# Two steps moved ahead of a wait in TensorE's order of an attention LSTM's turn

## The reference

```python
def attend(h):
    q = h @ Wq.T
    scores = jnp.einsum('bc,bsc->bs', q, context)
    alpha = jax.nn.softmax(scores, axis=-1)
    ctx = jnp.einsum('bs,bsc->bc', alpha, context)
    return jnp.tanh(jnp.concatenate([ctx, h], axis=-1) @ Wout.T + b_out)

def step(carry, x_t):
    h, c, attn = carry
    inp = jnp.concatenate([x_t, attn], axis=-1)
    gates = inp @ W_ih.T + b_ih + h @ W_hh.T + b_hh
    i, f, g, o = jnp.split(gates, 4, axis=-1)
    c = jax.nn.sigmoid(f) * c + jax.nn.sigmoid(i) * jnp.tanh(g)
    h = jax.nn.sigmoid(o) * jnp.tanh(c)
    out = attn_out = attend(h)
    return ((h, c, attn_out), out)
```

## Time and profile before

| | |
|---|---|
| median of 3 runs | 6059.23 us (6057.89 to 6060.78) |
| the profiled execution's own time | 6056.11 us |
| its span | 6054.3 us |
| PE busy | 5506.3 us, 91% of the span |
| PEld busy | 3879.1 us, 64% |
| DVE busy | 3606.7 us, 60% |
| ACT busy | 2103.8 us, 35% |
| POOL busy | 317.7 us, 5% |

### The profile page before, as it was taken

One profiled execution on the slowest core, in us unless ns is written; L12 is line 12 of the kernel. 1 busy time (PEld: TensorE's weight loads), 2 busy tenths in 40 slices (PEclk: granted clock), 3 DMA queues, 4 the chain that ended last, 5 costly groups with the idle time before them and its releaser, 6 DMA issues. The chain is left out here.

```text
span 6054.3 us, 385300 instructions
## 1 busy us (share of the span) xinstructions
PE 5506.3 (91%) x171736; PEld 3879.1 (64%) x171736; DVE 3606.7 (60%) x16290; ACT 2103.8 (35%) x8003; POOL 317.7 (5%) x779
## 2 busy tenths in 40 slices
PE   6899999999999999999999999999888879887989
PEld 2577777777777777777777777777644444444433
DVE  4355555555555555555555555555487898888831
ACT  3144444444444444444444444444222122223221
POOL 0000000000000000000000000000011111111000
PEclk8999999999999999999999999999899899899989
DMA  1100000000000000000000000000211101011111
GB/s 69 57 2 2 2 2 2 2 2 2 2 2 2 2 2 2 2 2 2 2 2 2 2 2 2 2 2 17 81 58 40 40 28 47 31 45 33 47 38 54
DMA packets 45135, 111.64 MB, mean 18 GB/s; under 512 B 8160, under 2 KB 10208, under 8 KB 44528
## 3 DMA queue, kind: packets, MB, share of 16 engines
q1 hardware_dynamic: 43600, 109.39, 5.6%
q10 hardware_dynamic: 1440, 1.06, 0.1%
HBM read 99.90 MB, written 10.52 MB: 18 GB/s over the span
## 5 line engine op out<-in xcount | busy, mean ns | idle before, releaser
L711 PE MATMUL lstm_part_ps<-lstm_keys,lstm_hid 128*4 128x128 f32 x32768 | 1024.1, 273 | 205.5 <-DVE lstm_hid L880 205.5
L727 PE MATMUL lstm_ctx_ps<-lstm_values,lstm_alpha 128*4 128x128 f32 (+1 forms) x49152 | 1051.4, 237 | 0.2 <-issue 0.2
L711 PEld LDWEIGHTS lstm_part_ps<-lstm_keys,lstm_hid 128*4 128x4 f32 x32768 | 771.3, 86 | 427.2 <-DVE lstm_hid L880 413.6
L727 PEld LDWEIGHTS lstm_ctx_ps<-lstm_values,lstm_alpha 128*4 128x4 f32 x49152 | 904.8, 86 | 90.7 <-issue 0.4
L909 DVE TENSOR_REDUCE lstm_neg_max<-lstm_part_ps 128x1 f32<-128x128 f32 x1024 | 299.1, 292 | 678.8 <-PE lstm_part_ps L711 678.8
L842 ACT ACTIVATE lstm_expo<-lstm_part_ps,lstm_neg_max 128x128 f32<-128x128 f32 x1024 | 376.4, 368 | 862.2 <-DVE lstm_neg_max L909 862.2
L670 PE MATMUL lstm_half_ps<-lstm_w_hid,lstm_hid 128*13 128x96 f32 x16384 | 596.0, 246 | 0.0
L862 DVE STREAM_TRANSPOSE lstm_gates<-lstm_half_ps 128x96 f32<-128x96 f32 x1026 | 290.1, 283 | 396.1 <-PE lstm_half_ps L670 372.0
L670 PE MATMUL lstm_half_ps<-lstm_w_attn,lstm_attn 128*13 128x96 f32 x16448 | 526.0, 248 | 0.0
L670 PEld LDWEIGHTS lstm_half_ps<-lstm_w_attn,lstm_attn 128*13 128x13 f32 x16448 | 300.5, 93 | 154.6 <-ACT lstm_attn L855 106.7
L1944 ACT ACTIVATE mix_gated<-mix_gate_ps 115x512 f32<-115x512 f32 (+2 forms) x200 | 112.6, 563 | 820.0 <-PE mix_gate_ps L1674 819.9
(11 more groups left out here) (336 smaller groups left out, 8593.0 us busy)
## 6 DMA issues: line engine op xcount, KB each, us to landing
mix_ring<-in_sm_chunks SPq DMA_DIRECT2D x120, 358.0 KB, 2.9
mix_ring<-in_mix_chunks SPq DMA_DIRECT2D x80, 384.0 KB, 3.0
lstm_xg<-xg_rows SPq DMA_DIRECT2D x514, 16.0 KB
xg_rows<-lstm_xg_tile SPq DMA_DIRECT2D x16, 512.0 KB, 2.6
ctxT<-in_ctxT SPq DMA_DIRECT2D x1, 2048.0 KB, 14.6
out_xT<-xT SPq DMA_DIRECT2D x4, 512.0 KB, 3.8
xT<-in_xT SPq DMA_DIRECT2D x1, 1536.0 KB, 9.8
lstm_w_x<-in_lstm_w_x SPq DMA_DIRECT2D x1, 1024.0 KB, 10.8
```

Of the source, the lines that this page charges most:

```text
L711: mm = pe.matmul(part_rows(score_ps[part], b), hid[:, k, lo:lo + SPACE], keys[:, k, b * SRC + c * P:b * SRC + (c + 1) * P], start=(n == 0 ...
L727: mm = pe.matmul(part_rows(ctx_ps[n], b), alpha[:, b, c, SPACE - 1 - c:2 * SPACE - 1 - c], values[:, b * SC + c, ctx_cols[n]], start=(c == ...
```

## The change

In `gates`, `half_attn(0, 1)` moves from behind `half_attn(1, 0)` to behind `half_attn(0, 0)`, and so ahead of the wait for `attn_ready[1]`. In the loop's body, `hidden_part()` moves from behind `turn(0)` to ahead of the wait for `exp_ready`. The instructions and their number stay the same, on all engines.

```diff
@@ -750,9 +750,9 @@
                     o_gate_x_hid(u)
                     pe.wait_ge(attn_ready[0], t + 1)
                     half_attn(0, 0)
+                    half_attn(0, 1)
                     pe.wait_ge(attn_ready[1], t + 1)
                     half_attn(1, 0).then_inc(half_ready[0], 1)
-                    half_attn(0, 1)
                     half_attn(1, 1).then_inc(half_ready[1], 1)
                     o_gate_attn()
 
@@ -783,9 +783,9 @@
                             scores(c, 0)
                         scores(2, 1)
                         scores(3, 1).then_inc(scores_ready, 1)
+                        hidden_part()
                         pe.wait_ge(exp_ready, 2 * t + 1)
                         turn(0)
-                        hidden_part()
                         half_hid(0, 0)
                         pe.wait_ge(alpha_ready, 2 * t + 1)
                         for n in range(PIECES):
```

## The result

The changed kernel takes 6080.13 us (median of 7 runs, 6078.34 to 6084.19) against 6059.23 us (7 runs, 6057.89 to 6060.78): ratio 1.0033, 95% interval 1.0024 to 1.0043. It is slower, by 20.9 us, or 0.041 us in each of the 512 turns. That lies in the range given (6040 to 6088), but not in its likeliest case, no change (6048 to 6071). The rival that said slower named the place rightly: a filler (a step put into an idle gap) makes the instruction behind it late.

The account below looks back on a forecast made before the run. The LSTM-with-attention loop, 512 turns of 7.73 us, was taken as the bound, followed along one turn's chain. Terms of 0 and +2.6 us added to the 6059.2 median gave 6061.8 us; 8-in-10 range 6040 to 6088.

Parts of the forecast that it names:

- no change: Whole kernel: the two moves cancel out within what a measurement can tell, 6048 to 6071 us; chance 0.60.
- The rival that said slower: At `turn(0)` and `half_attn(1, 0)`: filler outlasts its cover, from 0.024 us a turn; 6090 at 0.03 each; chance 0.23.
- Edit 1, 0 a turn: In `gates`, `half_attn(0, 1)` moved ahead of the wait for `attn_ready[1]`: second half and output gate earlier, nothing gained, 0 us.
- The rival that L867 had been held by the second transpose: VectorE's L867 waits for the second L862, not L831; part of the faster rival, 6028 to 6044 us, chance 0.15.
- The idle time only moves: TensorE's idle time goes from ahead of `turn(0)` to behind it, some 0.2 us a turn ahead of L727.
- The sign that I had set for being wrong on edit 2: Distance from the accumulator read's end to L886, 0.37 us before, changing by more than 0.02.
- No slack behind `turn(0)`: `turn(0)` releases copy L886, so any lateness delays the context, `turn(1)` and the rest of the turn equally.
- Edit 2, +0.005 a turn: `hidden_part()` moved ahead of the exponentials' wait: just fills the gap, `turn(0)` ends 0.005 us later, 2.6 us in all.
- The bound of +0.03: Upper bound per turn for moving `hidden_part()`, in us, from the last strip ending at 2005.37.
- saved start from rest: At `turn(0)`: 0.25 us from start to end, against 0.23 for `turn(1)` out of a busy array; refund offsets lateness.
- The start in the array's flow: Earlier matmuls delay the next by just what the array still has to do; `select(1)` starts at 2008.37, load at 2008.34.
- The strict order: `hidden_part`'s passes start one behind the other, `turn(0)` 0.395 us late, +202 us, 6261; chance 0.02.

Follow-up runs that it names:

- d_both_first: Kernel before, with `hidden_part()` and `half_hid(0, 0)` both moved ahead of the wait for the exponentials: 6145.63 us against 6057.37.
- b_hidden_only: Kernel before, with only `hidden_part()` moved ahead of the wait for the exponentials: 6076.69 us against 6057.37.
- c_halfhid_first: Kernel before, with `half_hid(0, 0)` instead of `hidden_part()` moved ahead of the wait for the exponentials: 6058.76 us against 6057.37.
- m_halfhid_narrow: Kernel before, with `half_hid(0, 0)` and the narrow pieces of `hidden_part` ahead of the exponentials' wait, wide ones behind `turn(0)`: 6146.32 us against 6060.69.
- l_halfhid_wide: Kernel before, with `half_hid(0, 0)` and the wide pieces of `hidden_part` ahead of the exponentials' wait, narrow ones behind `turn(0)`: 6131.13 us against 6060.69.
- a_gates_only: Kernel before, with only `half_attn(0, 1)` moved ahead of the wait for `attn_ready[1]`: 6056.67 us against 6057.37.
- g_spread: Kernel before, with `half_hid(0, 0)` ahead of the exponentials' wait and `half_hid(0, 1)` behind `hidden_part()`, before `select(0)`: 6043.50 us against 6060.69.

## Why the prediction was right or wrong, step by step

- **Edit 1, 0 a turn: right.** Alone it measures 0.9999, and the distances on the chain are as before (L862 starts 4.79 us after the first L842 in both kernels and L880 at 6.00, medians). The steps hold one by one: the first half is not late, although four rounds stand where two stood; the pair of transposes ends 0.16 us earlier and L835 0.11 nearer to L831; L880 does not move. The rival that L867 had been held by the second transpose is out: the transpose ends 0.12 us ahead of L867 now (2005.29 against 2005.41), and L867 still stands 0.04 behind L831's end.
- **The idle time only moves: right in kind.** L727 waits for L886. The forecast had some 0.2 us of it; it is 0.38 by the loads. The loads of the last filler now end at 2008.49 (2008.35 + 0.14), and until L727's at 2008.88 no load runs at all; I had counted by the matmuls' time in the array and left out that their loads are done earlier. The sign that I had set for being wrong on edit 2, a change of more than 0.02 us from the sum's end to L886, came: 0.41 instead of 0.37. The turn takes 7.78 us (the first L842 starts at 2007.79 and again at 2015.57), not 7.73 to 7.75.
- **No slack behind `turn(0)`: right.** The distances from L886 on are unchanged (0.22 to 0.23 to L727; 0.99 from the first copy to the second in every kernel, median), the copy follows the semaphore by 0.02 us everywhere, and lateness in `turn(0)` is paid in full: 0.172 a turn in `d_both_first`, where its matmuls start 0.17 late.
- **Edit 2, +0.005 a turn: this step failed.** It measures 0.038 alone and 0.034 to 0.041 wherever all of `hidden_part`, and nothing else, stands ahead of the wait. The place was the one named, work ahead of `turn(0)`; the size was mis-taken by 0.033, and the mechanism named, what a strip still has to do, does not give that size (see below). The bound of +0.03 was too low as well. That the range held the time is luck: edit 1 had a bound of its own that it did not use. I set the saved start from rest (0.01 to 0.02, read from 0.25 against 0.23 us of record length) against the last strip's 0.03. The runs show no such refund. The matmul rows could not have told: `turn(0)`'s recorded start is 0.51 us behind L842 with a late copy (`b_hidden_only`) and with a punctual one (`c_halfhid_first`), and its end is modelled. The semaphore updates do tell: 0.04 us more between the last pass's start and the update.
- **The start in the array's flow: right in part.** That a queue of earlier matmuls delays the next by what the array still has to do held at 0.17 us (`d_both_first`, `m_halfhid_narrow`) and at `select(1)`, where taking 8 passes out gave the forecast 15 us (17 measured). In `l_halfhid_wide`, which fills its fullest strips just as long, it was 0.138, and for the whole `hidden_part` alone it does not explain the loss.
- **The strict order.** By that rival, 6261 for the change; it was 6080, and with `half_hid(0, 0)` added still only 6146. The timeline of `l_halfhid_wide` shows passes that start ahead of earlier ones in the program. The rule of the Trainium skill, TensorE: Matmul & The Clock Gate, "Part 3: Packing small matmuls", that matmuls start and end in program order, does not hold here for the starts of passes in different column strips, and the measurement decides. On the ends the trace agrees: the semaphore of the fourth call came only behind the passes of earlier calls that had started later (2006.22).

What stays open is why the full `hidden_part` costs 0.034 to 0.041 us. Each of its parts alone costs 0.00, although it fills its strips just as long; all four strips together cost it, in either order. By the sum over a strip's work it should have been 0.00 to 0.03, and adding `half_hid(0, 0)` (0.165 in every strip) adds only 0.134: with it the lateness is in the starts of `turn(0)`'s passes (0.16), and the semaphore follows them by 0.23 instead of 0.26. Something that all four strips share when they are full would fit, but no run isolates it.

## What to carry to other kernels

Filling an idle gap of an engine brought nothing here, since the work that it took away stood on the chain nowhere else (`a_gates_only`, 0 us); ask who waited for it there, and move the filler that shortens a queue in front of a late wait (`g_spread`, -17 us), not the one that lay under cover already. A gap in front of an instruction without slack must be filled short of its length: here 0.165 us in all four strips was free, 0.215 in two of them was free, and 0.215 in all four cost 0.04, in a gap of 0.21. In a loop of 512 turns that is 20 us, and the starts and modelled ends of the matmul rows do not show it: look at the semaphore update, or at the first instruction that waits for it.

## What the hardware showed that I had not expected

- Matmul passes in different column strips overtake each other in their starts, not in their completion: in `l_halfhid_wide` four passes of a later step start from 2005.87 on, while four of `turn(0)`'s eight start at 2005.95 to 2005.99; the semaphore of `turn(0)`, though on an early pass, is updated at 2006.22.
- The lateness shows at the semaphore and the consumer, and hardly in the matmul rows: 0.26 us from the start of `turn(0)`'s last pass to the semaphore update instead of 0.22, and 0.35 us from its recorded start to L886 instead of 0.32.
- A 128x96 transpose that finds its input ready starts 0.20 us behind the one ahead of it (2005.04 against 2004.84) and shows 0.24 us instead of 0.28, so the pair takes 0.45 us instead of 0.61.
